# Local attention of two interleaved samples: scores that wait for their own key tile, and exponentials that open a step instead of closing one

## What is computed

```
q, k, v = jnp.split(qkv, 3, axis=-1)
q = l2norm(q) * qs
k = l2norm(k) * ksc
q, k = rotary_xpos(q, k)
...
bk, bv = (look_around(bk), look_around(bv))
sim = jnp.einsum('bhwid,bhwjd->bhwij', bq, bk)
sim = jnp.where(mask, -jnp.finfo(sim.dtype).max, sim)
attn = jax.nn.softmax(sim, axis=-1)
out = jnp.einsum('bhwij,bhwjd->bhwid', attn, bv)
```

## Time and profile before

| | value |
|---|---|
| median of three runs | 942.1 us |
| profiled execution, its own time | 944.34 us |
| its span, first to last instruction | 942.5 us |
| mean granted TensorE clock | 0.887 of 2.4 GHz |
| PE matmul busy | 741.4 us, 79% |
| DVE busy | 569.9 us, 60% |
| ACT busy | 540.3 us, 57% |
| POOL busy | 304.3 us, 32% |
| instructions | 15760 |

### The profile page before, as it was taken

The page is one execution under the profiler, slowest core; times in us unless marked ns, Lnnn a source line. Parts: engine busy times, 40 slices in busy tenths (PEclk is TensorE's granted clock), DMA queues, the critical chain, the costliest instruction groups (busy, mean ns, idle before and its releaser), DMA issues.

```text
span 942.5 us, 15760 instructions
## 1 busy us (share of the span) xinstructions
PE 741.4 (79%) x5368; PEld 481.8 (51%) x5368; DVE 569.9 (60%) x2212; ACT 540.3 (57%) x1349; POOL 304.3 (32%) x296
## 2 busy tenths in 40 slices
PE   5756688767596877779868778867778888888998
PEld 3434556445374646644435446445447465475443
DVE  4695455666566766747856644846646676583633
ACT  3436476474564624455586487587487674554542
POOL 3354323434333133143434412524412322321200
PEclk9877879998697987788988879989899898979999
DMA  8501010100100000111120111210111200103343
GB/s 267 158 0 41 13 41 1 40 13 12 40 2 12 1 1 1 39 39 54 35 73 23 46 51 29 57 40 1 45 43 33 56 13 24 28 13 93 93 113 94
DMA packets 37162, 41.83 MB, mean 44 GB/s; under 512 B 14345, under 2 KB 23771, under 8 KB 36955
## 3 DMA queue, kind: packets, MB, share of 16 engines
q1 hardware_dynamic: 37083, 40.83, 15.9%
HBM read 28.75 MB, written 2.62 MB: 33 GB/s over the span
## 4 chain that ended last, share of the span: by engine, by line
PE 40%; DVE 27%; ACT 19%; POOL 7%; issue 3%; DMA 1%; SPq 0%; DVEq 0%; POOLq 0%; ACTq 0%
ACT work L855 11%; PE moe_psum L616 4%; PE act_psum L606 4%; PE dve_psum L438 3%; PE act_psum L499 3%; PE dve_psum L715 3%; DVE work L1123 3%; DVE work L1146 2%; DVE stats L1092 2%; PE dve_psum L469 2%; PE dve_psum L509 2%; PE act_psum L768 2%; POOL v_loc L1554 2%; ACT v_loc L855 2%; DVE res_nrm L1101 2%
## 5 line engine op out<-in xcount | busy, mean ns | idle before, releaser
L855 ACT ACTIVATE work<-work,nbias,rnorm 128x128 f32<-128x128 f32 x256 | 122.6, 480 | 39.7 <-DVE nbias L1183 39.6
L1508 POOL TENSOR_TENSOR work<-work,rinv 128x512 f32<-128x512 f32 (+1 forms) x72 | 75.6, 1064 | 154.3 <-DVE rinv L1109 154.0
L438 PE MATMUL dve_psum<-wqkv,hTs 128*128 128x512 f32 x128 | 71.0, 682 | 21.1 <-ACT hTs L1003 19.4
L1548 POOL TENSOR_TENSOR hT<-hT,work 128x512 f32<-128x512 f32 x32 | 40.7, 1273 | 132.9 <-DVE work L1146 132.9
L1142 DVE TENSOR_TENSOR hT<-dve_psum,tab_a 128x512 f32<-128x512 f32 x32 | 22.0, 689 | 80.8 <-ACT res_nrm L866 37.8
L1123 DVE CUSTOM_DVE_ANT_0 work<-dve_psum,masks 128x128 f32<-128x128 f32 x256 | 58.6, 283 | 18.6 <-PE dve_psum L469 18.4
L1490 POOL TENSOR_SCALAR rstd<-mv 128x4 f32<-128x4 f32 x36 | 10.3, 286 | 176.3 <-DVE mv L1095 176.3
L838 ACT COPY hT<-act_psum 128x512 f32<-128x512 f32 (+1 forms) x60 | 31.1, 526 | 49.0 <-PE act_psum L499 25.4
L838 ACT COPY v_loc<-act_psum 77x512 f32<-77x512 f32 (+2 forms) x72 | 41.1, 580 | 30.6 <-PE act_psum L443 14.6
L457 PE MATMUL act_psum<-ident,v_loc 128*128 128x128 f32 x128 | 24.7, 329 | 36.9 <-POOL v_loc L1554 36.9
L469 PE MATMUL dve_psum<-kT,qT 64*64 64x128 f32 x1024 | 40.7, 305 | 10.8 <-DVE work L1146 7.3
(11 more groups left out here) (224 smaller groups left out, 2021.5 us busy)
## 6 DMA issues: line engine op xcount, KB each, us to landing
ahead<-cwT_dram SPq DMA_DIRECT2D x128, 64.0 KB, 2.1
v_loc<-v_loc SPq DMA_DIRECT2D x24, 256.0 KB, 3.7
kT<-cwT_dram SPq DMA_DIRECT2D x80, 64.0 KB, 2.1
qT<-cwT_dram SPq DMA_DIRECT2D x48, 64.0 KB, 2.0
wqkv<-in_wqkv_dram SPq DMA_DIRECT2D x2, 768.0 KB
res_nrm<-in_x_dram SPq DMA_DIRECT2D x4, 256.0 KB, 3.2
w_m<-in_w_m_dram SPq DMA_DIRECT2D x1, 1024.0 KB, 8.8
v_loc<-v_loc SPq DMA_DIRECT2D x8, 128.0 KB, 3.2
```

The costliest lines, as they stand in the source:

```text
L438: nc.tensor.matmul(bank[:], h, attn_w[:, k * INNER:(k + 1) * INNER], start=True, stop=True)\
L855: last = nc.scalar.activation(weights[:, i, :], weights[:, i, :], ACT.Exp, bias=nbias[u][:, b, i:i + 1], scale=scale_of(i), accum_out=sums ...
L1508: nc.gpsimd.tensor_tensor(some, some, by.unsqueeze(2).to_broadcast(list(some.shape)), ALU.mult).then_inc(ready[u], 1)
L1548: nc.gpsimd.tensor_tensor(own, own, partners[u][:, t % 2, k, :], ALU.add).then_inc(turned_ready[u], 1)
```

## The change

- PE: scores of tile t wait for the copies of query tile t and key tile t alone; before, the first waited for key tile 3. Scores of tile 0 stand in step 9 right behind `turn_q(3)`, those of tile 1 in step 10, and the turning of key tiles 2 and 3 behind them.
- ACT: step 9 has the copy of the last queries alone. Step 10 has `exp_local(0)` and then `take_k(2)` and `take_k(3)`. In the steps from 11 on `exp_local(n + 1)` stands first; before, `exp_local(n + 2)` stood last.
- DVE: `take_scores(0)` moves to step 9 and everything behind it by one step. Since `lprob` lies on the memory of `partners`, tiles 0 and 1 now wait until POOL has added the partners of tile t+2 (`turned_ready`). The wait for inverse norms is for the pair of tiles in question.
- POOL divides, and SP moves values, in the step that fits; each local attention has 16 steps in place of 17, so a sample has two steps fewer.
- Operations and their sizes are the same. Only ACT's table loads differ, as the order of the functions does.

```diff
@@ -66,7 +66,7 @@
 
 
 
-BODY_STEPS = 8 + LAYERS * (1 + 2 * TILES + 1 + 2 + TILES + 2 + 6) + 7 + CROSS_STEPS + 7 + 4
+BODY_STEPS = 8 + LAYERS * (1 + 2 * TILES + 2 + TILES + 2 + 6) + 7 + CROSS_STEPS + 7 + 4
 EXPERT_STEPS = (CHUNKS + 2) // PER_STEP + 1
 LEAD = 10
 TOGETHER = 8
@@ -458,8 +458,8 @@
                         last.then_inc(act_filled, 1)
 
                     def scores(t, u):
-                        if t == 0:
-                            pe.wait_ge(act_emptied, act_item["kT", l, TILES - 1, u] + 1)
+
+                        pe.wait_ge(act_emptied, max(act_item["qT", l, t, u], act_item["kT", l, t, u]) + 1)
                         banks = [dve_bank(("s_local", l, t, u, odd)) for odd in range(2)]
                         for c in range(INNER // P):
                             for half in range(2):
@@ -523,12 +523,12 @@
                             turn_k(0, u)
                         yield
                     turn_q(TILES - 1, u)
+                    scores(0, u)
+                    yield
+                    scores(1, u)
                     turn_k(2, u)
                     turn_k(3, u)
                     yield
-                    for n in range(2):
-                        scores(n, u)
-                        yield
                     for n in range(TILES + 1):
                         if n < TILES:
                             turn_probs(n, u)
@@ -904,19 +904,18 @@
                             take_k(0)
                         yield
                     take_turned(TILES - 1, u)
+                    yield
+                    exp_local(0, u)
                     take_k(2)
                     take_k(3)
                     yield
-                    for n in range(2):
-                        exp_local(n, u)
-                        yield
                     for n in range(TILES + 1):
+                        if n + 1 < TILES:
+                            exp_local(n + 1, u)
                         if n < TILES:
                             take_pt_hi(n, u)
                         if n >= 1:
                             take_out(n - 1, u)
-                        if n + 2 < TILES:
-                            exp_local(n + 2, u)
                         yield
                     yield
 
@@ -1170,6 +1169,9 @@
                     def take_scores(t, u):
                         mask = masks[:, 0 if t == 0 else 1, :]
                         b = t % 2
+                        if t < 2:
+
+                            dve.wait_ge(turned_ready[u], 2 * (TILES * l + t + 3))
                         for odd in range(2):
                             bank = filled(("s_local", l, t, u, odd))
                             for c in range(HALF):
@@ -1177,8 +1179,8 @@
                                 last = mask_and_peak(bank, c * KEYS, mask, lprob[u][:, b, i, :], peak[u][:, b, i:i + 1])
                             last.then_inc(dve_emptied, 1)
                             dve.wait_ge(dve_emptied, dve_item["s_local", l, t, u, odd] + 1)
-                            if t == 0:
-                                dve.wait_ge(rnorm_ready[u], 2 * (l + 1))
+                            if t % 2 == 0:
+                                dve.wait_ge(rnorm_ready[u], 2 * l + t // 2 + 1)
                             some = slice(HALF * odd, HALF * odd + HALF)
                             nc.vector.scalar_tensor_tensor(out=nbias[u][:, b, some], in0=peak[u][:, b, some], scalar=-1.0,
                                                            in1=rnorm[u][:, t, odd:HEADS:2], op0=ALU.mult, op1=ALU.mult)\
@@ -1704,10 +1704,11 @@
                         for t in range(TILES):
                             yield
                             yield
+                        yield
                         sp.wait_ge(act_filled, act_item["kT", l, TILES - 1, u] + 1)
                         shift_values(l, 0, v_early)
                         shift_values(l, 2, v_late)
-                        for _ in range(3 + TILES + 1):
+                        for _ in range(1 + TILES + 1):
                             yield
                         sp.wait_ge(dve_emptied, dve_item["attn_out", l, TILES - 1, u] + 1)
                         sp.dma_start(shifted[u][:, :, 0:half], y[u][:, :, 0:half]).then_inc(shift_done[u], 16)
```

## The result

The changed kernel takes 891.1 us (median of 4 runs, 889.2 to 894.9) against 942.1 for the kernel before: a ratio of 0.948, with an interval of 0.944 to 0.951. The profiled execution took 889.2 us with a span of 887.4, against 944.3 and 942.5. In the changed file the lines of ScalarE up to 855 keep their numbers, L1109 is now L1108, L1183 is L1185, and L1554 is L1555. In the rows TensorE is PE, VectorE DVE, ScalarE ACT and GpSimd POOL.

The account below looks back on a forecast made before the run. No engine was full, so time was taken as a sum of hand-overs between engines working in-order queues. 944.3 - 20.0 (kind 1) + 0 (kind 2) = 924.3 us; from the median 942.1, forecast 922, range 908 to 940.

Parts of the forecast that it names:

- Kind 1: Four places with slot 0 in attention and slot 1 projecting: 20.0 us gained, 5.6 of it in sample 0's layer 0.
- The other kind 1 places: Sample 0's layer 1 and sample 2's layers 0 and 1: exp(3) starts earlier, gains of 5.7, 5.5 and 3.2 us.
- Kind 2: Four places with slot 1 in attention and slot 0 in its feed-forward: little gained, taken as 0 together.
- upper bound: Most that each kind 2 place could gain, 4.1 us, if PE's wait for keys there is all path.
- The prediction's own sign of being wrong: Wrong if kind 2 moves its end by over 2 us, or kind 1's first place ends early without slot 1's projections.
- Table loads: ACT's exponentials lose four table loads in the program, 60 to 56, at 1.283 us each, 5.1 us in all.
- The cost that speaks against: In kind 1, DVE's `nbias` may stand for POOL's key normalisation: 0 to 3.5 us in all, half hidden.
- Costs at nothing: New waits of `scores` and `take_scores` are met by then; if their cover were gone, 1.02 us would show.
- Kind 2 gains too: Rival, chance 0.12: the keys' wait was path in kind 2 as well, 4 x 4.1 us more, about 906.
- The wait turns round: Rival, chance 0.18: DVE's `invert_sums` stands for its own step's exponential; half of kind 1's gain comes back, about 932.
- No change: Rival, chance 0.13: PE's projections and the other slot set attention's tails; early exponentials only lengthen waits, about 940.
- kind 2 gives it all back: Rival, chance 0.07: gelus between exp(0) and exp(1) are not recovered, 4 x 8.4 us lost, about 956.

Follow-up runs that it names:

- e5: Kernel before with only scores ahead of the last key turns and ScalarE's last key copies behind exp(0), 17 steps, exponentials closing their steps: 910.0 us.
- e12: Changed kernel with only ScalarE's copies of key tiles 2 and 3 back ahead of exp(0); TensorE's early scores stay: 911.0 us.
- e7: Changed kernel with scores(0) back behind the turns of key tiles 2 and 3 and those key copies ahead of exp(0): 911.0 us.
- e2: Kernel before with only ScalarE's exponentials moved, each opening the next step in place of closing its own: 917.5 us.
- e4: Changed kernel with one empty step per layer put back on every engine at the end of local attention: 890.5 us.
- e11: Changed kernel with each exp(n+1) moved from the step's opening to behind the copy of the own slot's probabilities: 909.0 us.

## Why the prediction was wrong

The direction was right and the size was not: 51 us for 20. By its own steps:

- **Kind 1, sample 0, layer 0.** The first and the last exponential came as worked out. The timeline of the changed kernel (start, us, operation, idle time ahead):

```profile
63.13 0.47 PE L457 MATMUL act_psum<-ident,v_loc 128*128 128x128 f32 x1 [3.01 <-POOL v_loc L1555]
```

```profile
63.13 0.50 ACT L855 ACTIVATE work<-work,nbias,rnorm 128x128 f32<-128x128 f32 x1 [3.42 <-DVE nbias L1185]
```

```profile
84.25 0.49 ACT L855 ACTIVATE work<-work,nbias,rnorm 128x128 f32<-128x128 f32 x1 [0.52 <-DVE nbias L1185]
```

  With the 4.0 us of the start added back, exp(0) stands at 67.1 (forecast 67.5) and exp(3) at 88.3 (87.9); it was 93.54. TensorE's wait ahead of L457 fell from 6.12 to 3.01 and not under 1, but the scores no longer stand behind it. Gain at exp(3): 5.2 us for 5.6. One link of the sum was luck: it ends exp(1) at 78.2 and adds 1.33 us a tile, which makes 79.5 for exp(2), and then says 82.6. The trace has 82.9 (78.85 and the 4.0), with ScalarE standing 3.12 us for slot 1's projection ahead of the squares in between.
- **The other kind 1 places, up to exp(3).** Counted from the start of their stage, exp(3) came 3.7, 4.5 and 3.3 us earlier (190.03, 466.82 and 592.58 with the shift of the stage's start, 15.7, 28.9 and 46.8, against 209.44, 500.22 and 642.68); forecast 5.7, 5.5 and 3.2. The four sum to 16.7 us, near the 20.0. In sample 0's layer 1 the forecast left the copy of the last queries at 182.81; it began at 169.45, which is 185.15 with the shift, and the exponentials are late by about that much (exp(0) at 187.5 for 185.5, exp(3) at 205.7 for 203.7).
- **The step that failed in kind 1: the sum stopped at exp(3).** The stages end 39.1 us earlier, so 22 us lie behind the start of exp(3), where the prediction put nothing: 7.8 and 7.7 of them in sample 0's layer 1 and sample 2's layer 0. I had costed ScalarE's queue only for the slot in attention. The rows of sample 0's layer 1 show what came behind it. Before:

```profile
213.97 0.69 DVE L1142 TENSOR_TENSOR hT<-dve_psum,tab_a 128x512 f32<-128x512 f32 x1 [3.54 <-ACT work L866]
...
217.17 0.23 DVE L1109 RECIPROCAL rinv<-sums 128x4 f32<-128x4 f32 x2
...
218.89 1.12 PE L479 MATMUL dve_psum<-ident,work 128*128 128x128 f32 x4 [2.92 <-POOL work L1508]
```

  and in the changed kernel:

```profile
193.99 0.18 DVE L1108 RECIPROCAL rinv<-sums 128x4 f32<-128x4 f32 x1 [0.95 <-ACT work L855]
...
194.84 0.60 PE L479 MATMUL dve_psum<-ident,work 128*128 128x128 f32 x4
```

  Before, slot 1's squares stood behind exp(3), its rotary multiplies behind the squares, and slot 0's own reciprocals behind the multiplies in VectorE's queue. They began 3.9 us after exp(3) had ended at 213.27, GpSimd's division behind them, and TensorE turned the last probabilities at 218.89. In the changed kernel the reciprocals stand ahead of slot 1's multiplies. From exp(3)'s start to that turn it is 9.45 us before and 4.81 after, 4.6 of the 7.8. Another 2.6 are clock: from 213.27 to 218.89 TensorE was busy for 1.13 us of 5.62, and its granted clock stood at 1.00 up to about 218 and at 0.50 for the products from 218.89 on, which took 5.65 us; the same products took 3.06 at a clock of 1.00 in the changed kernel. By parts, the step on its own gives 13.8 us in kind 1, the opening order 15.0, the keys 12.6, and together they give 39.1.
- **Kind 2.** "I take 0" is what failed: the four places gained 19.6 us, somewhat over the upper bound (4.1 a place, 16.4), and e5, the keys alone, gains 19.9 there. But the bound's reason, TensorE's stand for the keys, is not what the runs show. In e12 that stand is as short as in the changed kernel, and kind 2 gains only 10.2 us, as in e7 (10.6), which has no early scores; with ScalarE's key copies behind exp(0) it is 19.6. The term that was put at nothing is ScalarE's wait for the turned keys ahead of exp(0) (42.3 us in all, 7.1 in the changed kernel, 33.8 in e12). The opening order alone gains 12.0 in kind 2 as well (e2); how the two share the 19.6 stays open. Sample 1's layer 0 after:

```profile
111.02 0.48 ACT L855 ACTIVATE work<-work,nbias,rnorm 128x128 f32<-128x128 f32 x1
...
120.52 0.49 ACT L855 ACTIVATE work<-work,nbias,rnorm 128x128 f32<-128x128 f32 x1
...
131.20 0.58 ACT L1002 COPY hTs<-act_psum 64x511 f32<-64x511 f32 x1
131.80 0.49 ACT L855 ACTIVATE work<-work,nbias,rnorm 128x128 f32<-128x128 f32 x1
```

```profile
133.70 1.98 PE L438 MATMUL dve_psum<-wqkv,hTs 128*128 128x512 f32 x4
```

  Set against the same projection before:

```profile
148.92 3.05 PE L438 MATMUL dve_psum<-wqkv,hTs 128*128 128x512 f32 x4 [2.44 <-ACT hTs L1003]
```

  With the stage's shift of 11.4 us, exp(0) stands at 122.4, exactly as forecast; exp(1) at 131.9 (forecast 134.7), exp(3) at 143.2 (146.3; before 143.89), the end of `hTs` at 143.2 (146.3), the projection at 145.1 (148.6). So exp(1) was 5.7 us late and not 8.4, and it was all made up by exp(3). The forecast had slot 0's projection held by TensorE's turned probabilities; in the trace what held it before was `hTs` behind the closing exp(3), 2.44 us, and that wait is gone. The prediction's own sign of being wrong, that kind 2 moves its end by more than 2 us, came in all four places (3.5 to 6.1 us).
- **The clock.** The sum used each duration as the trace before had it. But in this stage 394 matmuls took 40.59 us before and 35.90 after, at a granted clock of 0.83 and 0.93, and the four products above 3.05 and 1.98 us. That is as much as the stage's whole gain, 4.3 us. Over the program it is 18.0 of 55.1 us. Whether the shorter waits are the whole reason for the clock was only argued from the two traces: no run set one against the other.
- **Table loads.** 60 to 56 came as forecast, but no run prices them alone: e4 has 60 and the changed kernel's time, with an empty step more.
- **The cost that speaks against** (`nbias` behind GpSimd, up to 3.5 us, and by the rule of the Trainium skill, SBUF — State Buffer, Who interferes with whom, a gain of 16.5 for 20) hardly came. At sample 0's layer 0 the `nbias` at 62.78 took 0.31 us for 0.16, up to about the end of GpSimd's first key product (62.03 and half of 2.04), and exp(0) was still 0.4 us earlier than worked out. The prediction called the row at 67.47 in agreement with the rule on two SBUF inputs; that row is a `tensor_scalar` with one input, so it does not bear on that rule, and the `nbias`, which has two, does.
- **Costs at nothing.** The new waits of scores and `take_scores` left no row among the waits; that stands.
- **Rivals.** ScalarE's 39.6 us for `nbias` fell to 8.4, as the forecast wanted (under 20). *Kind 2 gains too* (0.12, 906) was nearest. 906 was still 15 too slow, for kind 1's second half, and its reason, TensorE's path, is not the one that e12 shows, so its number in kind 2 was in part luck. *The wait turns round*: it did, from 13.8 to 50.3 us, twice what I expected, and did not keep the gain back; whether it costs anything by itself was not tried. *No change* and *kind 2 gives it all back* fell.
- **The range** (908 to 940) missed for that reason: it had a bound for a gain in kind 2 and none for what stood behind exp(3) in kind 1, through the other slot's squares and multiplies.

## What to carry to other kernels

On an engine that works one queue in order for several interleaved streams, ask of each instruction how long it stands at the head for its data and which ready work of the other streams is behind it. In this kernel the place for a long operation was a step's opening, where its data had mostly been there: the same exponential cost 18 us more behind one waiting copy (e11), and two short copies ahead of exp(0) cost all that TensorE's early scores bring (e12). When a sum is made for a move in such a queue, follow every stream to the end of its stage, and count the engines' waits that the move takes away in the stage of each. Parts of such a change do not add up (29, 26 and 7 us alone, 49 together, and 44 for the 29 and the 7), so run their combinations before you say what each is worth.
